# Two rings of PSUM banks and a new order of all queues in a six-layer local attention stack

## The reference

```python
WINDOW, HEADS, DIM_HEAD, QK_SCALE = 64, 16, 64, 8.0
def attn_layer(x, Wqkv, qs, ksc, Wo):
    q, k, v = split_heads(x @ Wqkv)                 # 256 -> 3 * 1024
    q = l2norm(q) * qs
    k = l2norm(k) * ksc
    q = q * cos * scale + rotate_half(q) * sin * scale
    k = k * cos / scale + rotate_half(k) * sin / scale
    out = local_attention(q, k, v)                  # each window of 64 sees itself and the one before
    return out @ Wo
def ffn_layer(x, g, bln, W1, b1, W2, b2):
    hg = (layernorm(x) * g + bln) @ W1 + b1         # 256 -> 2 * 682
    a, gate = split(hg)
    return a * gelu(gate) @ W2 + b2
for i in range(6):
    x = attn_layer(shift_tokens(x), ...) + x        # half of the columns come from the token before
    x = ffn_layer(shift_tokens(x), ...) + x
```

## Time and profile before

| | |
|---|---|
| median of 3 runs | 4240.27 us (4237.77 to 4240.35) |
| the profiled execution | 4244.68 us |
| its span (first to last instruction) | 4242.8 us |
| PE busy | 4056.7 us, 96% |
| DVE busy | 3104.7 us, 73% |
| ACT busy | 2683.5 us, 63% |
| POOL busy | 1965.6 us, 46% |
| mean granted TensorE clock | 0.974 |

### The profile page before, as it was taken

One profiled execution on the slowest core, in us unless ns is written; L12 is line 12 of the kernel. 1 busy time (PEld: TensorE's weight loads), 2 busy tenths in 40 slices (PEclk: granted clock), 3 DMA queues, 4 the chain that ended last, 5 costly groups with the idle time before them and its releaser, 6 DMA issues. The chain is left out here.

```text
span 4242.8 us, 98159 instructions
## 1 busy us (share of the span) xinstructions
PE 4056.7 (96%) x33244; PEld 2831.6 (67%) x33244; DVE 3104.7 (73%) x5354; ACT 2683.5 (63%) x7072; POOL 1965.6 (46%) x1355
## 2 busy tenths in 40 slices
PE   6999989999668999999999999999999999999997
PEld 3666545666345777777777777777777777777776
DVE  4888538886867777777777777777777777777774
ACT  3667535776525766666666666666666666666663
POOL 1000001000326666666666666666666665656662
PEclk8999998999779999999999999999999999999999
DMA  6111042221112000210011101110111100111001
GB/s 158 36 45 45 20 125 59 53 53 26 60 57 59 21 18 21 59 41 20 19 52 43 30 16 23 58 44 17 23 39 42 40 21 18 51 44 28 18 21 48
DMA packets 103314, 177.54 MB, mean 42 GB/s; under 512 B 27317, under 2 KB 61905, under 8 KB 102737
## 3 DMA queue, kind: packets, MB, share of 16 engines
q1 hardware_dynamic: 102096, 169.70, 14.9%
q0 software_dynamic: 768, 2.10, 0.4%
HBM read 94.93 MB, written 23.07 MB: 28 GB/s over the span
## 5 line engine op out<-in xcount | busy, mean ns | idle before, releaser
L2174 POOL TENSOR_TENSOR swp<-raw,table 128x512 f32<-128x512 f32 x384 | 480.8, 1274 | 636.5 <-DVE ss L2585 636.4
L938 DVE TENSOR_REDUCE maxima<-PS 128x1 f32<-128x512 f32 x1024 | 632.5, 681 | 122.8 <-PE PS L772 122.3
L2257 PE MATMUL PS<-wqk,xT 128*128 128x512 f32 x1536 | 688.1, 601 | 5.6 <-DMA wqk<-in_L_ffn_Wqkv 4.4
L2204 POOL TENSOR_TENSOR probs<-probs,prob_recip 128x512 f32<-128x512 f32 x384 | 475.8, 1257 | 432.5 <-DVE prob_recip L2643 432.4
L902 ACT ACTIVATE probs<-PS 128x512 f32<-128x512 f32 x1024 | 520.1, 603 | 154.9 <-PE PS L786 154.3
L2514 ACT ACTIVATE probs<-probs,neg 128x128 f32<-128x128 f32 x1536 | 595.9, 389 | 27.4 <-DVE neg L2637 25.8
L2184 POOL TENSOR_TENSOR rinv<-ssm,power 128x32 f32<-128x32 f32 x96 | 526.8, 5488 | 0.0
L2257 PEld LDWEIGHTS PS<-wqk,xT 128*128 128x128 f32 x1536 | 284.2, 190 | 337.0 <-issue 254.2
L2360 PE MATMUL PS<-xnT,w 128*128 128x128 f32 x3840 | 477.7, 276 | 0.4 <-DVE hidden L2703 0.4
L772 PE MATMUL PS<-k_stack,q_stack 112*128 112x512 f32 (+1 forms) x1024 | 430.4, 442 | 34.8 <-PEq L640 19.0
L2585 DVE TENSOR_REDUCE ss<-swp 128x16 f32<-128x1024 f32 x192 | 232.9, 1213 | 308.3 <-ACT swp L2465 308.3
(11 more groups left out here) (282 smaller groups left out, 8203.3 us busy)
## 6 DMA issues: line engine op xcount, KB each, us to landing
V_window<-V SPq DMA_DIRECT2D x180, 256.0 KB, 2.8
wqk<-in_L_ffn_Wqkv SPq DMA_DIRECT2D x12, 1024.0 KB, 6.5
w<-in_L_ffn_W SPq DMA_DIRECT2D x18, 640.0 KB
q_stack<-spin_qk SPq DMA_DIRECT2D x128, 80.0 KB
k_stack<-spin_qk SPq DMA_DIRECT2D x128, 80.0 KB
q_stack<-tok_qk SPq DMA_DIRECT2D x128, 64.0 KB, 2.7
k_stack<-tok_qk SPq DMA_DIRECT2D x128, 64.0 KB, 2.8
spin_qk<-shared SPq DMA_DIRECT2D x32, 256.0 KB
```

Source lines behind the costliest of these rows:

```text
L938: dve.tensor_reduce(maxima[:, k // 2, k % 2:k % 2 + 1], SM(r, k), AX.X, ALU.max).then_inc(sm_maxed, 1)
L2174: pool.tensor_tensor(swp[:, w, :, a:a + LD // 2], raw[:, w, :, b:b + LD // 2], table[:, j % 2, 2 + w, a:a + LD // 2].rearrange("p (o d) -> ...
L2204: pool.tensor_tensor(view, view, psr[:, 4 * q:4 * q + 4].rearrange("p (h o) -> p h o", o=1) .to_broadcast([P, 4, P]), ALU.mult).then_inc(p ...
L2257: mm = pe.matmul(wide(kind, half, j), xT[:, k, at:at + P], rhs, start=(k == 0), stop=(k == DC - 1))
```

## The change

Banks 0 to 3 become one ring (`W_JOBS`, four banks) for the projections, ffn_in and the scores, a bank for each of the four quarters of a tile's scores. Banks 4 to 6 become one ring of three (`T_JOBS`) for all transposes and for weigh's output. Bank 7 holds project_out's and ffn_out's results. The order and the lags of all five queues are new. No matmul, eviction or vector operation is added or removed. In take_x the waits for the third-last tile's projections now stand before every tile instead of every fourth.

```diff
-        WIDE = c.PS[:, 0:2, :]
-        ATT, FFN = c.PS[:, 2, 0:D], c.PS[:, 2, D:2 * D]
-        OUT = c.PS[:, 3, :]
-        TA, TD = c.PS[:, 4, :], c.PS[:, 5, :]
...
+        ATT, FFN = c.PS[:, 7, 0:D], c.PS[:, 7, D:2 * D]
...
+        W_JOBS = [("v", 0, 3), ("k", 1, 2), ("k", 0, 2), ("v", 1, 3), ("q", 1, 2), ("f", 2, 6), ("f", 0, 6), ("q", 0, 2), ("f", 1, 6), ("s", 0, 3), ("s", 2, 3), ("s", 1, 3), ("s", 3, 3)]
+        T_JOBS = [("xn", 0, 6), ("x", 0, 1), ("kt", 0, 3), ("p", 0, 4), ("kt", 1, 3), ("p", 1, 4), ("qt", 1, 3), ("qt", 0, 3), ("p", 2, 4), ("p", 3, 4), ("o", 0, 4), ("o", 1, 4)]
+        W_BANKS, T_BANKS = 4, 3
+        NARROW_JOBS = [("wo", 0, 5), ("w2", 0, 6)]
...
-                 ("s", 0): [masked[0], masked[1]], ("s", 1): [masked[2], masked[3]],
+                 ("s", 0): [masked[0]], ("s", 1): [masked[1]], ("s", 2): [masked[2]], ("s", 3): [masked[3]],
...
+        def bank_of(jobs, banks, first, kind, index, j):
+
+            at = [(k, x) for k, x, _ in jobs].index((kind, index))
+            return c.PS[:, first + (len(jobs) * (j + jobs[at][2]) + at) % banks, :]
...
                 def scores(tile, u):
...
-                    area_free(pe, SC_JOBS, "s", u, n)
+                    for w in range(2):
+                        area_free(pe, W_JOBS, "s", 2 * u + w, n, W_BANKS)
...
-                                out = SC(w)[v * WINDOW:(v + 1) * WINDOW, i, :]
+                                out = score_bank(2 * u + w, j)[v * WINDOW:(v + 1) * WINDOW, i, :]
...
                 def weigh(tile, u):
                     n, j, ly = tile
-                    area_free(pe, OUT_JOBS, "o", u, n)
+                    area_free(pe, T_JOBS, "o", u, n, T_BANKS)
+                    bank = turned("o", u, j)
...
                     if t4:
                         transpose_p(t4, 2)
+                    if t4:
+                        transpose_p(t4, 3)
+                    if t4:
+                        weigh(t4, 0)
+                    if t3:
+                        scores(t3, 0)
+                    if t3:
+                        scores(t3, 1)
+                    if t4:
+                        weigh(t4, 1)
                     if t6:
                         ffn_out(t6)
```

More of the change, by code:

```diff
@@ L2118, in step @@
                     if t1 and begins(t1):
[L2119 to L2123, removed]
+                        load_v(t1)
                     if t0 and begins(t0):
@@ L2126, in step @@
                     if t4 and begins(t4):
+                        load_ffn_in(t4)
+                    if t4 and begins(t4):
                         load_b1(t4)
                     if t0 and begins(t0):
[L2129 to L2139, removed]
+                        load_scales(t0)
+                    if t2:
+                        copy_v(t2)
                 steps(sp, step)
@@ L2250, in project @@
                     w = "qkv".index(kind)
-                    area_free(pe, W_JOBS, kind, half, n, banks=2)
+                    area_free(pe, W_JOBS, kind, half, n, W_BANKS)
                     pe.wait_ge(S[("w_q", "w_k", "w_v")[w]], 16 * ly + 16)
@@ L2352, in ffn_in @@
                     n, j, ly = tile
-                    area_free(pe, W_JOBS, "f", part, n, banks=2)
+                    area_free(pe, W_JOBS, "f", part, n, W_BANKS)
                     pe.wait_ge(S["xn_taken"], n + 1)
@@ L2532, in step @@
                 def step(t, i, l):
-                    t2, t3, t4, t6 = (stage(t, i, l, lag) for lag in (2, 3, 4, 6))
+                    t1, t2, t3, t4, t5, t6 = (stage(t, i, l, lag) for lag in (1, 2, 3, 4, 5, 6))
+                    if t5:
+                        take_o(t5, 0)
+                    if t1:
+                        take_x(t1)
+                    if t5:
+                        take_o(t5, 1)
                     if t4:
                         exponentials(t4, 0)
+                    if t2:
+                        take_qk(t2, 1, 1)
+                    if t6:
+                        take_xn(t6)
                     if t4:
                         exponentials(t4, 1)
-                    if t6:
-                        take_xn(t6)
+                    if t3:
+                        take_v(t3, 0)
+                    if t2:
+                        take_qk(t2, 1, 0)
+                    if t4:
+                        exponentials(t4, 2)
                     if t4:
@@ L2573, in step @@
                         take_k(t3, 1)
+                    if t6:
+                        gelu(t6, 0)
+                    if t4:
+                        take_p(t4, 1)
+                    if t2:
+                        take_qk(t2, 0, 0)
+                    if t4:
+                        take_p(t4, 3)
                 steps(act, step)
@@ L2714, in step @@
                     t1, t2, t3, t4, t5, t6 = (stage(t, i, l, lag) for lag in (1, 2, 3, 4, 5, 6))
-                    if t2:
-                        normalise(t2, 0)
+                    if t6:
+                        gate(t6, 1)
+                    if t3:
+                        take_q(t3, 1)
+                    if t5:
+                        moments_ready(t5)
+                    if t3:
+                        take_q(t3, 0)
+                    if t5:
+                        aggregate(t5)
+                    if t2:
+                        sum_squares(t2, 0)
+                    if t5:
+                        variance(t5)
+                    if t6:
+                        gate(t6, 0)
+                    if t4:
+                        take_p(t4, 2)
+                    if t2:
+                        floor_squares(t2)
+                    if t5:
+                        standardise(t5)
+                    if t3:
+                        mask_scores(t3, 0)
+                    if t3:
+                        mask_scores(t3, 1)
+                    if t3:
+                        mask_scores(t3, 2)
+                    if t3:
+                        maxima(t3, 0)
+                    if t3:
+                        maxima(t3, 1)
+                    if t2:
+                        add_sines(t2, 1)
+                    if t6:
+                        finish(t6)
+                    if t3:
+                        maxima(t3, 2)
+                    if t3:
+                        mask_scores(t3, 3)
+                    if t2:
+                        cosines(t2, 0)
+                    if t3:
+                        invert_sums(t3, 0)
+                    if t3:
+                        maxima(t3, 3)
                     if t2:
@@ L2719, in step @@
                     if t1:
[L2720 removed]
+                        sum_squares(t1, 1)
+                    if t4:
+                        residual(t4)
                     if t2:
[L2722 to L2730 removed]
```

278 lines of the change are left out of this document (102 added, 176 removed).

## The result

The kernel after takes 4199.7 us (median of 4 runs, 4197.7 to 4202.9), the kernel before 4240.0: a ratio of 0.9905, 95% interval 0.989 to 0.992. It is faster by 40 us where 58 were forecast. The profiled execution took 4199.7 us with a span of 4197.8.

The account below looks back on a forecast made before the run. PE was taken to bound the kernel, busy for 2742.00 of 2742.00 us in the steady part. 4240.3 less 58 (96 x 0.6) with fill and drain unchanged gave 4182, range 4150 to 4215.

Parts of the forecast that it names:

- The bound and the switches: PE bounds the local layers' steady part; fewer array-mode switches per step save 58 us over 96 tiles (29 to 86).
- Four switches fewer at 0.15 make 0.6 us: PE's step: array-mode switches fall from eight to four, 0.15 us each, shortening the 30.40 us step to 29.8.
- Nothing saved: Rival: the added time belongs to any block change among small tiles, or refilling; step stays 30.4, time 4240; chance 0.05.
- The inner switches: PE's two switches between weighing (128*64) and scores (64*64): taken at 0.15 us each, none between scores 0 and 1.
- free: Rival on PE's weighing-scores switches: they cost nothing, saving 0.9 us a step, 86 us in all, 4154.
- dear: Rival on PE's weighing-scores switches: each costs 0.29 us, saving only 0.3 us a step, 29 us in all, 4211.
- No late hand-over: Every chain from ACT and DVE to PE has 0.7 us or more slack; late rival 4326, chance 0.11.
- Slack 0.9: ACT's run reaches take_p 1 0.9 us early; gate 0 is done at 23.6, before scores 1 at 24.5.
- 0.7: Slack in us of DVE's own chain to gate 0, done with hand-over at 23.8, ahead of scores 1 on PE.
- Decides 1.3 beyond the rows: Late gate 0 holding up scores 1 on PE decides from 0.6 us of lateness, 1.3 beyond the rows; chance 0.11.
- Filling and draining: PE's idle time at the pipeline's two ends, 26 us together, taken as unchanged, with -12 to +12 us.
- PE without idle time in the steady part: Forecast sign in the profile after: PE never idles in the local layers' steady part, with steps of 29.8 us.

Follow-up runs that it names:

- Experiment 3: The kernel after with transpose_p 3 moved from in front of weighing 0 to between weighing 0 and scores 0: 4214.9 us, ratio 0.994 to before.
- Experiment 4: The kernel after with ffn_out's 42-row part at its beginning, next to weigh 1, instead of its end: 4186.0 us, ratio 0.988 to before.
- experiment 5: The kernel after with two extra DVE reductions in front of sum_squares 0, making gate 0 late: 4304.3 us, ratio 1.015 to before.
- experiment 9: The kernel after with sixteen more fulfilled waits heading PE's local-layer program, moving the loop's head by 8 instructions: 4180.1 us, ratio 0.986 to before.
- experiments 9 to 11: The kernel after with 16, 256 and 512 more waits on PE, moving the loop's head by 8, 128 and 256 instructions: 4180.1, 4192.5 and 4215.2 us.
- experiment 1: The kernel after with PE's loop jump moved from behind ffn_out to behind projections v0, k1, k0, same engine order: 4185.5 us, ratio 0.987 to before.
- experiment 7: After's two bank rings with the orders and lags of the kernel before on all five queues: 4246.2 us, ratio 1.0015 to before.

## Why the prediction was right in part

By its own steps:

- **The bound and the switches: right.** "Four switches fewer at 0.15 make 0.6 us", 58 us in all; measured 0.61 in three steps of four and 0.70 in every fourth, 61. Experiment 3 puts one switch at 0.15 by itself, and 4 shows the same price at a place that the change never touched. "Nothing saved" falls with them.
- **The inner switches: right.** From the last group of weighing to the scores 3018.87 - 3018.66 = 0.21 pass where the pitch is 0.117: 0.09, as in the earlier trace rows. The sixteen groups of scores take 1.91 against 1.74 at 0.109: 0.05 for the start and about 0.1 for the end, and nothing between scores 0 and scores 1. Neither free nor dear. The Trainium skill's rule (TensorEngine Tiling (Array Packing), Key Properties) that a change of mode drains and another tile of the same mode doesn't fits both kinds in this trace, 0.09 us from weighing to the scores and nothing between the two scores. Experiment 4 adds that a chain with 42 rows in it pays for a change as well.
- **No late hand-over: right, with the slack too small.** "Slack 0.9" and "0.7" for gate 0 are 1.4 in the trace (gate 0 ends at 2267.14, scores 1 starts at 2268.6) and 1.3 by experiment 5; take_p 2 has 1.0 as foretold (2268.49 to 2269.53). "Decides 1.3 beyond the rows" was near the truth, and the price behind it, a microsecond of step for a microsecond of lateness, is what experiment 5 shows. ACT idles 5.4 us on average before take_x, 3.1 before take_p 3 and DVE 2.4 before sum_squares 1, as foretold.
- **Filling and draining: right.** 4 us saved, inside the 12 either way.
- **The step that failed: there was no term for the loop's jumps.** The sum took every tile at the steady step, and the forecast of the profile said "PE without idle time in the steady part"; it has 14.4 us. But the new order also moved what stands at both ends of PE's loop body. Before, project v, ffn_out and transpose_p 0 stood ahead of the jump, and 4.1 us of them were queued against the 3.4 to 3.8 us of the branch. After, weigh 1 and ffn_out stand there, and 3.3 us are queued against 3.8 to 4.0. That costs 0.8 to 1.0 us at each jump (3.5 in all; 3.1 in experiment 9, where nothing comes on top), and this much belongs to the order. The other 21 us are the second fetch and the half clock behind it, and they belong to the place where the loop's head came to lie (experiments 9 to 11). The earlier trace rows could not show any of it, because PE's busy time had no gap before. The branch's row in the trace of before (median 3638 ns) could have; the prediction never looked at what hid it.

With the head moved by 8 instructions the change gives 4180.1, and the prediction said 4182. So near a hit has luck in it: the steps save 61 and not 58, and the jumps, which the sum left out, still take 3.1 of it.

## What to carry to other kernels

Where an engine that sets the time runs a loop, read the branch's row in its sequencer and what is queued when it starts: put the cut where more than 4 us of long matmuls are queued (4.1 hid branches of up to 3.8 here, 3.3 didn't). If a stall follows a few instructions behind the jump, move the loop's head by some instructions before you blame the order. Put blocks of small tiles side by side, and look for short rows hidden in whole-array chains; padding them with zeros saved more here (0.34 us of a step) than half of what the change took from it (0.61).

## What the runs showed of the hardware

- A taken branch of PE lasts 3.3 to 4.2 us and an untaken one 76 ns. The Trainium skill gives about 108 ns for a compare-and-branch (Advanced Engine Details and Errata, Control Flow Timing); for the taken ones the measured time decides.
- ACT stands 17.4 us at its own four jumps (its row of waits above) in after, and 17.2 in experiment 1, with its branch at 45 ns. There PE never waits for it; in experiment 7 it may be what PE's waits of up to 0.6 us come from.
- After the idle stretches of 2.3 to 2.9 us in after (0.8 to 1.0 us and two transposes ahead of them) PE ran at 1.2 GHz, granted clock 0.50 from 2122 to 2127 us; in experiment 4 it did so at two jumps and stayed at 2.4 at the other two, behind 2.33 and 2.61 us (granted clock 1.00 from 2599 to 2609 and from 3558 to 3564 us). After 0.5 to 0.8 us alone (experiment 9) it stayed at 2.4.
- POOL's product for the rotation takes 1.71 us on average where it took 1.27 before, and DVE's cosine product 1.57 where the earlier trace rows has 1.20: the new order lets the two run side by side. That this is why was only argued; it cost nothing, since both have room.
